# The last stage of a convolution and spectral kernel: four neighbouring image rows in a partition, and x1 kept by image

## What is computed

```
x1  = x  + filtered_lrelu(groupnorm(x))              # up by 2, leaky relu, down by 2
out = x1 + irfft2(contract(rfft2(groupnorm(x1))))    # 64 modes each way, low-rank weights
```

## Time and profile before

| | |
|---|---|
| median of three runs | 5974.37 us (5970.19 to 5981.99) |
| the profiled execution | 5977.58 us, span 5975.8 us |
| PE busy | 5432.6 us, 91% of the span |
| DVE, ACT, POOL busy | 72%, 58%, 40% |
| DMA packets | 587,637, 562.23 MB |

### The profile page before, as it was taken

One profiled execution on the slowest core, in us unless ns is written; L12 is line 12 of the kernel. 1 busy time (PEld: TensorE's weight loads), 2 busy tenths in 40 slices (PEclk: granted clock), 3 DMA queues, 4 the chain that ended last, 5 costly groups with the idle time before them and its releaser, 6 DMA issues. The chain is left out here.

```text
span 5975.8 us, 192820 instructions
## 1 busy us (share of the span) xinstructions
PE 5432.6 (91%) x75424; PEld 4915.4 (82%) x75424; DVE 4316.1 (72%) x6707; ACT 3483.7 (58%) x6349; POOL 2377.4 (40%) x2566
## 2 busy tenths in 40 slices
PE   8989989899899898998974999999999999996888
PEld 6778778777777777777764999999999999996888
DVE  7868878788687787887866777777777777762323
ACT  6757757577476675765732666666666666652222
POOL 6747747477475574764720222222222222210000
PEclk9999999999899999999986999999999999998989
DMA  1131121311212213113141222121212121219999
GB/s 51 55 89 55 58 87 51 93 48 56 89 55 69 76 48 97 48 55 90 55 145 57 63 64 64 62 66 60 69 58 69 57 70 56 70 50 348 348 347 317
DMA packets 587637, 562.23 MB, mean 94 GB/s; under 512 B 15092, under 2 KB 540276, under 8 KB 574196
## 3 DMA queue, kind: packets, MB, share of 16 engines
q1 hardware_dynamic: 587124, 554.87, 28.6%
HBM read 286.38 MB, written 268.44 MB: 93 GB/s over the span
## 5 line engine op out<-in xcount | busy, mean ns | idle before, releaser
L1177 DVE TENSOR_TENSOR Ml<-ring,Mh 128x1024 f16<-128x1024 f32 x1024 | 1230.2, 1222 | 546.8 <-ACT Mh L1144 546.7
L1144 ACT ACTIVATE Mh<-ring 128x1024 f16<-128x1024 f32 x1024 | 1027.7, 1023 | 420.2 <-PE ring L1080 412.2
L243 POOL TENSOR_TENSOR Y<-Yf,Y 128x532 f16<-128x532 f32 x1024 | 1210.7, 1196 | 133.0 <-ACT Y L477 90.7
L1079 PE MATMUL ring<-wcur,b_hi 128*128 128x128 f16 x8192 | 1006.8, 219 | 85.0 <-POOL wcur L1034 74.5
L1080 PE MATMUL ring<-wcur,b_lo 128*128 128x128 f16 x8192 | 1005.7, 219 | 0.0
L1079 PEld LDWEIGHTS ring<-wcur,b_hi 128*128 128x128 f16 x8192 | 800.2, 99 | 113.1 <-POOL wcur L1034 74.6
L277 PE MATMUL ring<-uth,A 128*128 128x266 f16 x6144 | 821.7, 284 | 34.9 <-issue 18.5
L1080 PEld LDWEIGHTS ring<-wcur,b_lo 128*128 128x128 f16 x8192 | 802.0, 98 | 29.7
L1091 PE MATMUL ring<-xs,Mh 128*128 128x32 f16 x8192 | 783.3, 219 | 1.0 <-DVE Ml L1177 1.0
L1093 PE MATMUL ring<-xs,Ml 128*128 128x16 f16 x8192 | 778.3, 208 | 0.6 <-issue 0.6
L277 PEld LDWEIGHTS ring<-uth,A 128*128 128x128 f16 x6144 | 614.6, 100 | 195.6 <-issue 31.2
(11 more groups left out here) (138 smaller groups left out, 9592.4 us busy)
## 6 DMA issues: line engine op xcount, KB each, us to landing
xb<-in_x SPq DMA_DIRECT2D x128, 512.0 KB, 4.4
x<-x1b SPq DMA_DIRECT2D x64, 1024.0 KB, 6.3
spec<-sp_out SPq DMA_DIRECT2D x256, 256.0 KB, 2.6
xin<-spec SPq DMA_DIRECT2D x128, 512.0 KB, 6.4
fd<-ft SPq DMA_DIRECT2D x128, 512.0 KB, 4.0
F<-fd SPq DMA_DIRECT2D x8, 8192.0 KB, 27.6
xq<-x SPq DMA_DIRECT2D x128, 512.0 KB, 5.3
out<-xq SPq DMA_DIRECT2D x64, 1024.0 KB, 8.2
```

What stands on the lines that cost most here:

```text
L243: pool.tensor_tensor(Y[:, e, 1, m], Yf[:, m], Y[:, e, 0, m], ALU.subtract).then_inc(e_yl, 1)
L1079: pe.matmul(o, b_hi[:, z, 8 * u + k, :], wcur[:, z, 0, :], start=True, stop=False)
L1144: act.activation(hi, ps, ACT.Copy).then_inc(e_hi, 1)
L1177: dve.tensor_tensor(lo, ps, hi, ALU.subtract).then_inc(e_lo, 1)
```

## The change

It touches where rows lie, in SBUF and in DRAM. In stage 3 a partition gets four neighbouring rows of one image of the quad instead of one row of each of four images: partition (i, a) holds rows 4a to 4a+3 of image i, which lie together in out, 2 KB. To get there, ScalarE's copy to zb picks every fourth row of its PSUM bank, so that zb is (r, image, a), and each of `final`'s four matmuls takes one r in place of one image. x1 in DRAM becomes (image, row, column), like out. So stage 1 stores it in pieces of 512 B (one row), and stage 3 loads it in pieces of 2 KB, where it loaded 4 KB (eight images' parts of one row). The number of DMAs, their sizes and their order stay.

```diff
+ROWS = 4
 # phase1
+        x1_v = x1.rearrange("g h w -> h g w")
-                sp.dma_start(x1[:, bass.ds(16 * h, 16), :],
+                sp.dma_start(x1_v[:, bass.ds(16 * h, 16), :],
                              x1b[:, 4 * par:4 * par + 4].rearrange("p q i w -> p (q i) w")).then_inc(x1_st[par], 16)
 # phase3
-        zb = sb("zb", [128, 2, IMGS * H])
-        xq = sb("xq", [128, 4, HALF * IMGS, W])
+        zb = sb("zb", [128, 2, ROWS, IMGS, H // ROWS])
+        xq = sb("xq", [128, 4, HALF, ROWS * W])
-        out_v = out.rearrange("b c h w -> h (b c) w")
+        x1_v = x1.rearrange("(q i) (a r) w -> (i a) q (r w)", i=IMGS, r=ROWS)
+        out_v = out.rearrange("b c h w -> (b c) h w").rearrange("(q i) (a r) w -> (i a) q (r w)", i=IMGS, r=ROWS)
-                    sp.dma_start(xq[:, e, 8 * n:8 * n + 8, :],
-                                 x1[:, bass.ds(16 * h + 8 * n, 8), :]).then_inc(r_ld, 16)
+                    sp.dma_start(xq[:, e, 2 * n:2 * n + 2, :],
+                                 x1_v[:, bass.ds(4 * h + 2 * n, 2), :]).then_inc(r_ld, 16)
-                sp.dma_start(out_v[:, bass.ds(16 * h, 16), :], xq[:, e]).then_inc(o_st[e % 2], 16)
+                sp.dma_start(out_v[:, bass.ds(4 * h, 4), :], xq[:, e]).then_inc(o_st[e % 2], 16)
-                for m in range(IMGS):
-                    mm = pe.matmul(ring[:, 4 + k % 4, 128 * m:128 * m + 128], zb[:, k % 2, 128 * m:128 * m + 128], iy[:],
+                for m in range(ROWS):
+                    mm = pe.matmul(ring[:, 4 + k % 4, 128 * m:128 * m + 128],
+                                   zb[:, k % 2, m].rearrange("p i a -> p (i a)"), iy[:],
                                    start=True, stop=True)
-                act.activation(zb[:, k % 2, :], ring[:, k % 4, :], ACT.Copy).then_inc(e_z, 1)
+                act.activation(zb[:, k % 2].rearrange("p r i a -> p r (i a)"),
+                               ring[:, k % 4].rearrange("p (g r) -> p r g", r=ROWS), ACT.Copy).then_inc(e_z, 1)
-                    x_ = xq[:, k // 4, 4 * (k % 4):4 * (k % 4) + 4, :].rearrange("p i w -> p (i w)")
+                    x_ = xq[:, k // 4, k % 4, :]
 # program
-    x1 = nc.dram_tensor("x1", (H, B * C, W), F32, kind="Internal").ap()
+    x1 = nc.dram_tensor("x1", (B * C, H, W), F32, kind="Internal").ap()
```

## The result

The changed kernel takes 5993.89 us (median of six runs, 5990.51 to 6005.1) against 5974.74: 1.0032 times the kernel before, 95% interval 1.0019 to 1.0045. It is 19 us slower, a small difference, but the interval doesn't reach 1; forecast was 32 us faster, and the time lies 32 us above the range of 5920 to 5962. The profiled execution took 5990.51 us, its span is 5988.7.

A forecast was written before the change was run, and what follows sets the result against it. TensorE was taken to pace stage 3 between 8 MB F loads, with waits behind those loads. Six waits 5.3 us shorter, 31.8 + 0.9 - 0.15 = 32.5 us, brought 5974.4 to 5942 us, range 5920 to 5962.

The forecast's parts named there:

- Stores of out: Stage 3: stores in 2 KB instead of 512 B pieces run at 385 for 285 GB/s, 2.7 for 3.65 us a MB.
- The straight line: Time of a DMA piece against its size, drawn through 512 B (285 GB/s) and 16 KB (428); gives 385 GB/s for 2 KB.
- Loads of x1: Stage 3: pieces shrink from 4 KB to 2 KB, so 1 MB takes 2.7 for 2.6 us, 0.15 us more.
- 3.5 us a MB: Sign of a wrong prediction: loads of x1 in stage 3 taking over 3.5 us a MB.
- address pattern: Stage 3 loads of x1: 128 neighbouring pieces instead of rows 512 KB apart; called better but priced at zero.
- One step of SP: Stage 3, one x1 load plus one store of out: transfers and 0.15 us overhead sum to 5.6 us, for 6.39 measured.
- A: Stage 3, from an image's end to the landing of x1 behind the 8 MB F load: 33.6 us falls to 28.3.
- SP's lateness: SP reaches an image's end late, having waited for a landing; this goes, 1.5 us on average over six images.
- the six waits: TensorE's stage 3 waits for VectorE after the first: each falls from 12.85 to 7.5 us, 31.8 us in all.
- The rival "slower": 2 KB pieces run no faster than 512 B, a step takes 7.5 us, DMA paces stage 3: 6019 us; chance 0.05.
- Clock, start, end: Half-clock loss of 2.2 us a wait and the first F's wait stay; first landing moves 0.15 us, last store shortens 0.9.
- ScalarE and stage 1: The zb copy with a step of four, and stage 1's x1 stores in 512 B pieces (77 us engine time, covered): zero.

The follow-up runs named there:

- before_load_2k: The kernel before with only its stage 3 loads of x1 cut into 2 KB pieces, same addresses: 1.0004 times the kernel before.
- loads_overlap: The changed kernel, but SP issues the next x1 load without waiting for the last to land, up to two steps in flight: 5953.73 us, 0.996 of the kernel before.

## Why the prediction was wrong

- **Stores of out.** Right in kind: 385 GB/s forecast for 2 KB, 407 to 414 in the stretches of the store. Wrong for the 512 B that they replace: inside a step these run at 345 to 349 GB/s, not at the 285 of the lone last store. So 1 MB goes from 3.0 to 2.6 us of the engines, half of the 0.9 us that was counted on. The straight line itself holds: through 512 B at 347 GB/s and 16 KB at 428 it gives 385 for 1 KB and 407 for 2 KB (estimates from these rows), and 381 to 386 and 407 to 414 were measured.
- **Loads of x1.** Right for the pieces (0.12 us in before_load_2k for 0.15), wrong for the load. "The line gives ... 2.7 us for 2 KB" is the price of a load alone (4.3 us to landing, 403 GB/s); behind 2 KB stores it runs at 183 to 208 GB/s for its first 3 us and lands after 5.8 us. That is over the 3.5 us a MB which the prediction itself named as a sign that it is wrong. For the address pattern it took zero, and for 2 KB pieces that is right (stage 3 takes 607.7 us with them apart, 606.2 with them together); what it had no term for is that loads in 4 KB blocks suffer far less behind these stores (590.3).
- **One step of SP: this is the step that failed.** "Today 2.6 + 3.65 = 6.25 us of transfer stand against the measured 6.39, so 0.15 us is overhead." SP issues a load when the last one has landed; the step is a load's round trip, and the store's own time isn't a term of it. The quicker store was worth nothing there, and what it did to the load cost 0.7 us a step. The agreement was chance, in two ways. With the store at its own 3.0 us the sum is 5.6 us, and the 0.15 us of overhead would have been 0.8. And today's step lies near the engines' limit as well: with overlapping loads it is still 6.18 us at a DMA share of 1.05 to 1.08, so a share of 1.03 couldn't tell which of the two limits held.
- **A, and the sum.** Everything after followed from steps of 5.6 us. SP's lateness was read wrongly too: the landing it waited for came at 5694.79 us, 0.2 us before the image's end, and what made SP late was the issuing of the load, 1.77 us. With 7.08, six steps are 42.5 us, more than the 38.4 that TensorE takes, SP comes later, and the six waits grow from 12.85 to 15.7 us ((102.2 - 8.3) / 6, the first wait being 8.3 us) instead of falling to 7.5. The rival "slower" had the right form (it decides from a step of 6.65 us on) and the wrong cause, as the 2 KB pieces are quick. Where the transfers don't wait for each other's landing (loads_overlap), a step that VectorE doesn't hold up takes 5.48 us for the 5.6, from F to F it is 68.2 us for the 66.7 that A's arithmetic gives, and the median is 5953.7 for 5942: the second half of the argument was sound.
- **Clock, start, end.** The first wait stayed (29.9 for 30.2 us). The last store gained 0.4 us, not 0.9: 5.1 us to landing for 5.5.
- **ScalarE and stage 1.** Both right at zero: 597 ns, the same for the read with a step of four as for the read in order (the argument from "a slope of 0.83 ns an element" didn't show it, since two rows always lie on one line); x1's stores land after 6.8 us (6.3 before) where 8.2 was allowed for, and stage 3 doesn't start later.

Not settled: where the stores' bytes stand in the way of the loads. The runs show that it grows with the bytes and with the size of the pieces, that loads of 4 KB pieces in one block suffer less of it than others, and that it fades when loads overlap. The later landing of out's stores (8.6 for 8.2 us) adds nothing: each is issued behind a load that lands 0.5 us later itself. Whether the bytes wait in the memory or on the way to it was not tried. Why 4 KB loads take 6.72 us a step in one block and 6.95 when spread, while 2 KB ones show no such difference, is open too.

## What to carry to other kernels

Before pricing a faster transfer, find out what its queue waits for, first in the chain of work that ended last: if each load is issued when the last one has landed, the period is that load's round trip, a quicker store beside it is no term of it, and it can make the load slower. Test for it by taking the stores away or by letting two loads be in flight, before believing a sum of transfer times that happens to match the period. Larger pieces pay where the engines are really full, here 60 GB/s and 78 us once loads overlapped and the 8 MB load no longer stood in the way.

## What the hardware showed that I had not expected

- Loads of 512 KB from DRAM land in 4.3 us when nothing is stored, in 5.3 with stores of 1 MB in 512 B pieces between them, and in 5.8 with 2 KB pieces.
- The DMA share stood at 1.03 to 1.07 with 4 KB loads and 512 B stores at 325 to 352 GB/s, and at 1.04 with 412 GB/s in larger pieces: a share of 1 says nothing of the bytes.
- Behind the same 2 KB stores, loads of 4 KB pieces in one block cost TensorE 85.4 us of waits, loads of 4 KB pieces 512 KB apart 99.3, loads of 2 KB pieces 102.2 and 103.2.
- Stores of 1 KB and 2 KB pieces moved at the rates that a straight line through 512 B (347 GB/s, inside a step) and 16 KB (428) gives, to 2%; the lone last store, at 285, was no guide.
